# Gelu's inner polynomial: an ACT square and one fused DVE step for two POOL products and a DVE step

## The chip, the cores and the metric

The kernel runs on one core of a Trainium2 chip. The metric is the device time of one execution in microseconds; lower is better. The engines of the core are named as in the profile: PE (TensorE, matmuls), DVE (VectorE), ACT (ScalarE), POOL (GpSimd) and SP (SyncE, which issues the DMAs). Each runs its own queue of instructions in order, and they wait for each other by semaphores.

## The reference, cut to what matters

Sixteen sequences of 512 tokens of width 128 pass a causal attention with 16 heads of 8, a residual and a layer norm. Then a router picks 63 of the 512 tokens of each sequence; for them alone a second attention and a gelu MLP run, the results go back to their places, and a second layer norm ends it. The change touches only the gelu of that MLP, in its tanh form:

```python
def _gelu(x):
    return jax.nn.gelu(x, approximate=True)
...
        x1 = x_sel + o
        x2 = x1 + jax.nn.gelu(rmsnorm(x1, ln2) @ w1) @ w2
```

With h = rmsnorm(x1, ln2) @ w1, the gelu is 0.5 h (1 + tanh(sqrt(2/pi) (h + 0.044715 h^3))). The inner polynomial is h + 0.044715 h^3 = h (1 + 0.044715 h^2).

## The kernel before

The sixteen sequences are batches, taken two by two as eight pairs. One pass of the main loop is one pair and has 16 slots, 8 groups of heads for each batch of the pair. In a slot ACT takes the Tanh of one group's scores in two units out of PSUM (L708) and the Exp of the group before (L723); POOL multiplies the Exp's diagonal blocks by a triangle, the causal mask (L619, two instructions per group); PE computes the scores one group ahead (L1170) and, when four groups are masked, their products with v (L1187), which are also what frees the buffers of `pr` that the Exp writes. `pr` holds five groups, and six from pair 3 on (`SIX_FROM`, L43; the wait is at L720).

Everything else is fitted into these slots from order lists written out by hand, one for each engine (`PE_ORDER`, `VE_ORDER`, `POOL_ORDER`, `ACT_ORDER`), with two entries per slot. An entry such as `att.hh@-2` is a step of the pair two passes back. `run_side` (L479) issues them. The stages are `prep` (transposes, q, k, v and their norms, for the batch ahead), `fin` (the end of the first attention), `route`, `sel` (gather of the chosen tokens), `att` (second attention and the MLP up to the gelu) and `late` (second matmul of the MLP, scatter, last norm, for a pair up to three passes back). With the last groups of scores the first loop is empty, and the last two pairs' `sel`, `att` and `late` remain.

The steps around the change, in the order of their data:

- `att.w1` on PE (L1371) writes h to PSUM; `att.h` on DVE copies it to `hb` (L1079).
- `att.hh` on POOL: `hq` = h h. It is the first of two entries of slot 8 in POOL's list (L155), behind that slot's causal mask.
- `att.hp` on DVE: `hq` = 0.044715 `hq` + 1 (L1083). In DVE's list it stands behind `att.h` and behind `late.root2`, the four small steps L803 to L806 on the 128x8 tile `lo_v` (L134).
- `att.hu` on POOL: `hu` = `hq` h. It waits too for the second matmul of the pair before (`late.w2`), which reads `hu`.
- `att.tanh` on ACT (L694), in slot 9 behind the two Tanh units and ahead of the Exp (L175): `hq` = tanh(sqrt(2/pi) `hu`).
- `att.g` on DVE (L1087): `hu` = (`hq` + 1) h; then `late.w2` on PE (L1378) and `late.proc` on DVE (L1093, L1095).

Between `att.hp` and `att.g` DVE has `prep.qk1` (L825), `route.w` (L918, L919) and `late.norm` (eight steps, L1113); behind `att.g` come `route.row`, `route.win` (L934), `route.coef` (L956, L958), `fin.yU1`, `late.proc`, and `prep.v`, the copy of v (L836). POOL's product `prep.sq` on the next batch (`st<-qk`) follows two slots after `att.hu`. `hq` shares its memory with the tile `sc`, under whose name the profile lists it; all of POOL's plain products have the line L621.

## Time and profile before

| | us |
|---|---|
| runs | 793.32, 791.93, 792.43 |
| median | 792.43 |
| profiled execution | 795.73 |
| its span, first to last instruction | 793.9 |
| PE busy | 650.0 |
| DVE busy | 596.5 |
| ACT busy | 553.3 |
| POOL busy | 386.2 |

The busy time of an engine is the sum of its instructions; the span holds a start of some 40 us, in which weights come in and the first batch is prepared, some 650 us in which groups of scores run, and some 105 us at the end without scores. Idle time in front of an instruction is listed with the instruction that ended it. An engine's idle time matters only where the chain of work that ended last passes through it, so the chain is read beside the waits.

### The profile page before, as it was taken

The page shows a single profiled execution, that of the slowest core. Times are in us where ns is not written, and L with a number is a line of the kernel's source. Part 1 is how long each engine was busy: PE and PEld are TensorE (multiplying, and loading weights), DVE is VectorE, ACT ScalarE, POOL GpSimd, SP SyncE. Part 2 cuts the span into 40 slices and gives each one's busy share as a digit, 9 for nine tenths or more (in the row PEclk, how much of TensorE's full clock was granted, in tenths as well). Part 3 has the DMA queues.
Part 4 walks back from the last instruction along what each step waited for, and adds up shares of the span by engine and source line. Part 5 has one row for each costly group of instructions (what it writes and reads, how often), then busy time and mean ns, then how long its engine had stood idle before and what let it go on. Part 6 is the DMA issues. An engine that isn't in the chain of part 4 may idle for free.

```text
span 793.9 us, 16532 instructions
## 1 busy us (share of the span) xinstructions
PE 650.0 (82%) x6384; PEld 373.9 (47%) x6384; DVE 596.5 (75%) x1649; ACT 553.3 (70%) x403; POOL 386.2 (49%) x399
## 2 busy tenths in 40 slices
PE   3387777889989998999989998999899979855742
PEld 2243323455546454555546454545464546344432
DVE  3651636765897889888988898788998887687656
ACT  0399887786988798879788978788798969500000
POOL 5244545536555475556646564556547653511210
PEclk9558667778989998899889988898999878965755
DMA  6303030405230323040412121030303040000001
GB/s 199 67 2 80 12 69 1 81 2 107 81 80 2 69 66 82 28 67 15 66 44 53 30 53 55 19 64 4 64 28 68 2 68 28 14 1 28 0 1 53
DMA packets 97855, 36.72 MB, mean 46 GB/s; under 512 B 69090, under 2 KB 95090, under 8 KB 97778
## 3 DMA queue, kind: packets, MB, share of 16 engines
q1 hardware_dynamic: 97778, 35.67, 20.4%
q8 instruction: 51, 0.84, 0.4%
q14 instruction: 26, 0.21, 0.1%
HBM read 14.69 MB, written 4.19 MB: 24 GB/s over the span
## 4 chain that ended last, share of the span: by engine, by line
PE 45%; DVE 27%; ACT 12%; issue 9%; POOL 4%; DMA 2%; SPq 1%; DVEq 0%; ACTq 0%; POOLq 0%
PE ps_y L1187 15%; PE ps_s L1170 10%; ACT pr L723 8%; ACT th L708 4%; PE ps_m L1286 3%; DVE wins L934 2%; POOL pr L619 2%; DVE qn_v L842 2%; PE ps_m L1371 1%; PE ps_a L1236 1%; PE ps_a L1218 1%; DVE v_aug L836 1%; DMA k_st<-st 1%; PE ps_m L1270 1%; PE ps_m L1194 1%
## 5 line engine op out<-in xcount | busy, mean ns | idle before, releaser
L708 ACT ACTIVATE th<-ps_s 128x1024 f32<-128x1024 f32 (+1 forms) x256 | 278.6, 1129 | 77.1 <-PE ps_s L1170 67.5
L619 POOL TENSOR_TENSOR pr<-pr,tri 128x320 f32<-128x320 f32 (+1 forms) x256 | 188.2, 757 | 192.9 <-ACT pr L723 192.8
L723 ACT ACTIVATE pr<-th 128x2304 f32<-128x2304 f32 x128 | 271.5, 2122 | 8.7 <-PE ps_y L1187 8.4
L1170 PE MATMUL ps_s<-q_st,k_st 32*64 32x512 f16 (+7 forms) x2048 | 190.8, 315 | 42.5 <-ACT th L708 34.6
L1187 PE MATMUL ps_y<-pr,v_aug 128*32 128x512 f32 (+7 forms) x2048 | 171.6, 469 | 7.8 <-POOL pr L619 7.6
L1170 PEld LDWEIGHTS ps_s<-q_st,k_st 32*64 32x64 f16 x2048 | 92.1, 114 | 168.0 <-issue 63.5
L633 POOL TENSOR_TENSOR st<-qk,st 128x1024 f16<-128x1024 f32 x32 | 76.7, 2417 | 49.5 <-DVE st L852 49.5
L1187 PEld LDWEIGHTS ps_y<-pr,v_aug 128*32 128x32 f32 x2048 | 58.3, 116 | 76.7 <-issue 47.6
L621 POOL TENSOR_TENSOR k_wide<-qkT,head_of 128x1024 f32<-128x1024 f32 x16 | 30.1, 1901 | 41.6 <-DVE qkT L1017 41.6
L694 ACT ACTIVATE sc<-hu 128x512 f32<-128x512 f32 x8 | 5.0, 630 | 64.3 <-POOL hu L621 64.3
L934 DVE SCALAR_TENSOR_TENSOR wins<-w_wide,x,later 128x512 f16<-128x512 f32 (+1 forms) x64 | 41.2, 644 | 2.6
L690 ACT ACTIVATE pm<-pm 128x1008 f32<-128x1008 f32 x8 | 8.3, 1043 | 41.9 <-DVE pm L1031 41.9
L621 POOL TENSOR_TENSOR z_base<-x,coef 128x512 f32<-128x512 f32 x16 | 17.1, 1067 | 41.4 <-DVE coef L958 41.4
L621 POOL TENSOR_TENSOR r<-x,rw_row 128x512 f32<-128x512 f32 x16 | 18.9, 1181 | 35.5 <-DVE x L910 35.5
L621 POOL TENSOR_TENSOR st<-qk 128x1024 f32<-128x1024 f32 x16 | 30.3, 1893 | 5.9 <-DVE qk L825 5.7
L825 DVE COPY qk<-ps_a 128x512 f32<-128x512 f32 x16 | 10.7, 666 | 28.9 <-PE ps_a L1218 28.9
L1286 PE MATMUL ps_m<-mask_a,E 128*64 128x512 f32 x112 | 31.0, 605 | 0.0
L1348 PE MATMUL ps_a<-vv,k_wide 128*128 128x32 f32 x128 | 19.7, 315 | 9.2 <-DVE v_aug L836 5.7
L860 DVE STREAM_TRANSPOSE y_u<-ps_y 128x512 f32<-128x512 f32 x32 | 22.6, 705 | 5.8 <-PE ps_y L1187 5.8
L1218 PE MATMUL ps_a<-wT,xT 128*128 128x256 f32 x64 | 25.1, 532 | 0.0
L1348 PEld LDWEIGHTS ps_a<-vv,k_wide 128*128 128x128 f32 x128 | 18.9, 234 | 11.1 <-issue 6.9
L825 DVE COPY qk<-ps_m 128x512 f32<-128x512 f32 x16 | 11.1, 691 | 14.7 <-PE ps_m L1218 14.6
(224 smaller groups left out, 1074.0 us busy)
## 6 DMA issues: line engine op xcount, KB each, us to landing
x_in<-in_L_attn_x SPq DMA_DIRECT2D x16, 256.0 KB, 3.5
x_res<-in_L_attn_x SPq DMA_DIRECT2D x16, 256.0 KB, 2.8
result<-y_out SPq DMA_DIRECT2D x16, 256.0 KB, 2.2
mask_a<-in_L_ffn_attention_mask SPq DMA_DIRECT2D x3, 1024.0 KB, 5.4
pr<-in_L_ffn_attention_mask SPq DMA_DIRECT2D x2, 1024.0 KB, 7.9
w_sb<-in_L_ffn_w SPq DMA_DIRECT2D x2, 256.0 KB
q_st<-st SPq DMA_TRANSPOSE x16, 4.5
k_st<-st SPq DMA_TRANSPOSE x16, 4.8
```

The lines of the kernel that those rows point to most:

```text
L619: return nc.gpsimd.tensor_tensor(buf, buf, tri[:, None, :].to_broadcast([P, blocks, 64]), ALU.mult)
L621: mul = lambda out, a, b: nc.gpsimd.tensor_tensor(out, a, b, ALU.mult)
L633: pl["prep"].done(nc.gpsimd.tensor_tensor(lo_parts[s], qk_twice[s], hi_parts[s], ALU.subtract), f"lo_{part}", b)
L708: nc.scalar.activation(th[:, gi % 2, c0:c1], ps_s[:, c0:c1], ACT.Tanh, scale=1.0 / (QK_SCALE ** 2 * DH ** 0.5 * SOFTCAP))\
L723: nc.scalar.activation(pr[:, probs_at(n):probs_at(n) + GROUP], th[:, gi % 2, :], ACT.Exp, scale=SOFTCAP).then_inc(exp_done, 1)
L860: ve["fin"].done(nc.vector.transpose(y_u[:, half], ps_y[:, :]), f"yU{half}", b)
L934: step(lambda: nc.vector.scalar_tensor_tensor(won[c], w_wide[:, P * c:], x1[:, k, c, D:D + 1], later[:, 0:n], ALU.is_le, ALU.mult, accum_o ...
L1170: last = mm(ps_s[64 * s:64 * s + 64, COL[kb]:COL[kb] + S - 64 * kb], k_st[rows, k, gi // 2, 64 * kb:64 * kb + 64], q_st[rows, k, gi // 2, ...
L1187: last = mm(ps_y[32 * j:32 * j + 32, 64 * kb:S], v_aug[:, k, kb, gi, :], pr[:, c:c + S - 64 * kb], start=(kb == 0), stop=(kb == NB - 1), s ...
L1218: last = mm(at(f"prep.qk{i}", b)[:, :].rearrange("p (n t e) -> p n t e", t=2, e=32)[:, :, t % 2], xT[:, P * t:P * t + P], wT[:, 0:2, :].re ...
L1286: last = mm(at("sel.R")[SLOTS * k:SLOTS * k + SLOTS, :], E[:, c, SLOTS * k:SLOTS * k + SLOTS], (mask_b if k and q < 2 else mask_a)[:, c, : ...
L1348: last = mm(at("att.PV")[:, 32 * n:32 * n + 32], PT[:, n, :], vv[:, n, :, :].rearrange("p k c -> p (k c)"), start=True, stop=True)
```

## The change

The two POOL steps `hh` and `hu` and the DVE step `hp` are taken out. ACT gets a step `sq` in slot 9, directly ahead of its Tanh: `hq` = Square(h), as soon as `h` is there. DVE gets a step `u` where `hp` stood: `hu` = (`hq` + 1/0.044715) h, one instruction, which waits for the square and, as `hu` did on POOL, for the second matmul of the pair before. The factor 0.044715 goes into the scale of the Tanh. No other entry of an order list is moved.

```diff
     "att": ["sc0", "mx0", "sub0", "sc1", "mx1", "sub1", "den", "rden", "PT0", "PT1", "o0", "o1", "oT", "x1f",
-        "ss2"] + rsqrt_of("r2", 1) + rsqrt_of("r2", 2) + ["hn2", "h2T", "h", "hp", "g"],
+        "ss2"] + rsqrt_of("r2", 1) + rsqrt_of("r2", 2) + ["hn2", "h2T", "h", "u", "g"],
     "late": ["x2", "proc", "z0", "z1"] + moments_of(2 * NT, "_") + rsqrt_of("ln_", 1) + rsqrt_of("ln_", 2) +
...
     "sel": ["zb0", "zb1"],
-    "att": ["kw0", "kw1", "hh", "hu"],
+    "att": ["kw0", "kw1"],
 }
...
     ["att.root1@-2", "route.rank/0@-1"], ["prep.qk0/0@1", "att.root2@-2", "att.hn@-2", "fin.root2/1@-1"],
-    ["att.h2T@-2", "fin.x1/1@-1", "fin.yU0/0@0"], ["att.h@-2", "late.root2@-3", "att.hp@-2"],
+    ["att.h2T@-2", "fin.x1/1@-1", "fin.yU0/0@0"], ["att.h@-2", "late.root2@-3", "att.u@-2"],
     ["prep.qk1/0@1", "route.w/1@-1"], ["late.norm@-3", "att.g@-2", "route.row/1@-1", "route.win/1@-1"],
...
     ["route.xw/1@-1"], [],
-    ["att.hh@-2"], ["att.hu@-2"],
+    [], [],
     [], [],
...
     [], [],
-    [], ["att.tanh@-2"],
+    ["att.sq@-2"], ["att.tanh@-2"],
     [], [],
...
         gate_ready = sem("gate_ready")
+        square_ready = sem("square_ready")
         turned = [sem(f"turned{i}") for i in range(2)]
...

-            def att_hh(q, _):
-
-                ve["att"].wait(pool, q, "h")
-                pl["att"].done(mul(hq[:, :], hb[:, :], hb[:, :]), "hh", q)
-
-            def att_hu(q, _):
-                pe["late"].wait(pool, q - 1, "w2")
-                ve["att"].wait(pool, q, "hp")
-                pl["att"].done(mul(hu[:, :], hq[:, :], hb[:, :]), "hu", q)
-
-            table = {"prep.sq": prep_sq, "prep.lo": prep_lo, "route.xw": route_xw, "sel.zb": sel_zb, "att.kw": att_kw,
-                     "att.hh": att_hh, "att.hu": att_hu}
+            table = {"prep.sq": prep_sq, "prep.lo": prep_lo, "route.xw": route_xw, "sel.zb": sel_zb, "att.kw": att_kw}

...

+            def att_sq(q, _):
+                ve["att"].wait(act, q, "h")
+                nc.scalar.activation(hq[:, :], hb[:, :], ACT.Square).then_inc(square_ready, 1)
+
             def att_tanh(q, _):
-                pl["att"].wait(act, q, "hu")
-                nc.scalar.activation(hq[:, :], hu[:, :], ACT.Tanh, scale=float(np.sqrt(2.0 / np.pi)))\
+                ve["att"].wait(act, q, "u")
+                nc.scalar.activation(hq[:, :], hu[:, :], ACT.Tanh, scale=float(0.044715 * np.sqrt(2.0 / np.pi)))\
                     .then_inc(gate_ready, 1)

-            table = {"att.exp": att_exp, "att.tanh": att_tanh}
+            table = {"att.exp": att_exp, "att.sq": att_sq, "att.tanh": att_tanh}

...

-            def att_hp(q, _):
-                pl["att"].wait(v, q, "hh")
-                ve["att"].done(nc.vector.tensor_scalar(hq[:, :], hq[:, :], 0.044715, 1.0, ALU.mult, ALU.add), "hp", q)
+            def att_u(q, _):
+                v.wait_ge(square_ready, q + 1)
+                pe["late"].wait(v, q - 1, "w2")
+                ve["att"].done(nc.vector.scalar_tensor_tensor(hu[:, :], hq[:, :], 1.0 / 0.044715, hb[:, :], ALU.add, ALU.mult),
+                               "u", q)

...
                      "att.oT": att_oT, "att.x1f": att_wo, "att.ss": att_squares, "att.hn": att_hn, "att.h2T": att_h2T,
-                     "att.h": att_w1, "att.hp": att_hp, "att.g": att_gate, "late.proc": late_w2,
+                     "att.h": att_w1, "att.u": att_u, "att.g": att_gate, "late.proc": late_w2,
                      "late.z0": lambda q, _: late_sc(q, 0), "late.z1": lambda q, _: late_sc(q, 1), "late.ln": late_ln,
```

## Rows read from the trace of the kernel before

**Rows 1.** The page: busy us, share of the span and instructions of each engine

```profile
PE 650.0 (82%) x6384; PEld 373.9 (47%) x6384; DVE 596.5 (75%) x1649; ACT 553.3 (70%) x403; POOL 386.2 (49%) x399
```

**Rows 2.** Busy time by stretch, from gelu Tanh to gelu Tanh, pairs 2 and 3

```profile
core 0: us, PE busy (x) PEld busy (x) DVE busy (x) ACT busy (x) POOL busy (x), PEclk, DMA share, GB/s
...
408.50:490.40 81.90, 76.05 (x801) 43.81 (x805) 71.82 (x205) 68.61 (x50) 47.07 (x47) 0.90 0.21 47
490.40:574.50 84.10, 75.97 (x805) 43.07 (x805) 72.75 (x205) 68.62 (x51) 47.05 (x47) 0.90 0.19 42
```

**Rows 3.** Busy time by stretch, around the gelu Tanh of pairs 2 and 4

```profile
406.00:416.70 10.70, 10.70 (x144) 5.68 (x145) 10.00 (x31) 7.98 (x7) 4.65 (x6) 0.91 0.18 54
...
571.50:582.40 10.90, 10.07 (x141) 5.61 (x141) 10.43 (x31) 7.72 (x6) 5.06 (x6) 0.99 0.17 50
```

**Rows 4.** Groups of ACT by line and form: busy us, mean ns | idle before, releaser

```profile
L723 ACT ACTIVATE pr<-th 128x2304 f32<-128x2304 f32 x128 | 271.5, 2122 | 8.7 <-PE ps_y L1187 8.4
...
L694 ACT ACTIVATE sc<-hu 128x512 f32<-128x512 f32 x8 | 5.0, 630 | 64.3 <-POOL hu L621 64.3
...
L708 ACT ACT_TABLE_LOAD x1 | 1.3, 1283 | 0.0
```

**Rows 5.** The instructions on tile `sc` (`hq`): duration ns min/median/max, first and last start

```profile
L621 POOL TENSOR_TENSOR sc<-hb x8: 1029/1037/1042, 241.3 to 773.0; 128x512 f32<-128x512 f32 x8
L1083 DVE TENSOR_SCALAR sc<-sc x8: 420/420/427, 242.3 to 774.4; 128x512 f32<-128x512 f32 x8
L621 POOL TENSOR_TENSOR hu<-sc,hb x8: 1261/1267/1277, 242.8 to 775.0; 128x512 f32<-128x512 f32 x8
...
L1087 DVE SCALAR_TENSOR_TENSOR hu<-sc,hb x8: 677/684/691, 244.8 to 777.8; 128x512 f32<-128x512 f32 x8
```

**Rows 6.** The same view of tile `lo_v`, a step of `late.root2`

```profile
L804 DVE SCALAR_TENSOR_TENSOR lo_v<-lo_v x8: 166/963/1035, 323.5 to 788.4; 128x8 f32<-128x8 f32 x8
```

**Rows 7.** Timeline of pair 2: start us, us, engine, line, what [idle before <-releaser]

```profile
404.38 0.69 DVE L1079 COPY hb<-ps_m 128x512 f32<-128x512 f32 x1 [1.06 <-PE ps_m L1371]
...
408.32 0.23 DVE L919 TENSOR_SCALAR x<-x,rb 128x4 f32<-128x4 f32 x1
...
408.46 2.14 DVE L1113 TENSOR_SCALAR y_out<-y_out,mv,lo_v 128x128 f32<-128x128 f32 x8
408.54 0.63 ACT L694 ACTIVATE sc<-hu 128x512 f32<-128x512 f32 x1 [3.50 <-POOL hu L621]
...
411.26 1.87 POOL L619 TENSOR_TENSOR pr<-pr,tri 128x320 f32<-128x320 f32 x2 [2.75 <-ACT pr L723]
...
416.69 1.41 DVE L836 COPY v_aug<-ps_m 64x512 f32<-64x512 f32 x2 [0.23 <-PE ps_m L1226]
416.88 1.89 POOL L621 TENSOR_TENSOR st<-qk 128x1024 f32<-128x1024 f32 x1
```

**Rows 8.** The chain that ended last, in pairs 0, 2 and 4: start, us, what

```profile
242.82 1.28 POOL hu L621
...
415.57 1.10 PE ps_m L1226 x32
...
573.18 1.29 POOL hu L621
```

**Rows 9.** The same chain in pairs 6 and 7, around the gelu

```profile
720.35 1.05 DVE lo_v L804
...
722.76 0.80 DVE x L919
...
773.04 1.05 DVE lo_v L804
...
774.82 3.02 DVE y_out L1113 x8
```

**Rows 10.** Timeline of pairs 2 and 3 where PE waits for `yT`

```profile
425.16 2.05 PE L1236 MATMUL ps_a<-wT,yT 128*128 128x128 f32 x8 [0.71 <-DVE yT L875]
...
505.94 0.85 DVE L801 TENSOR_TENSOR sel_v<-sel_v 128x1 f32<-128x1 f32 x1
...
508.10 2.05 PE L1236 MATMUL ps_a<-wT,yT 128*128 128x128 f32 x8 [1.75 <-DVE yT L875]
```

## The prediction

> **What bounds the kernel now.** I read the engines' busy times first [rows 1]: no engine is full over the whole span, PE comes nearest with 82%. So I cut the span into pairs of batches, from one gelu Tanh to the next [rows 2]. In a steady pair PE is busy 76.05 of 81.90 us, ACT 68.61, DVE 71.82, POOL 47.07. The reader should see that PE leads, that ACT has some 13 us to spare and that POOL is half empty.
>
> Then the piece that the change touches. ACT sits idle in front of every gelu Tanh: 64.3 us over eight pairs, and POOL's `hu` product ended the wait [rows 4]. In a steady pair it is 3.50 us [rows 7]. The naive reading is that eight such waits are there to be won. The next view speaks against it: from 406.0 to 416.7, which begins inside the stall of pair 2, PE is busy 10.70 of 10.70 us [rows 3]. PE has score groups computed ahead and other work to do, and does not notice that ACT stands still. The chain of work that ended last says the same: there it runs through PE (the `v` matmuls at 415.57) and not through `hu` [rows 8]. It passes through `hu` in only two of the first six pairs, pair 0 (242.82) and pair 4 (573.18) [rows 8], and in pair 4 PE does have holes, 10.07 busy of 10.90 [rows 3]. In the last two pairs no scores are left, the chain runs step by step on DVE, and there the gelu is on it [rows 9].
>
> **The change part by part.** Removed per pair: POOL's `hh` (1037 ns) and `hu` (1267 ns), DVE's `hp` (420 ns) [rows 5]. Added: on ACT a Square over 128x512, on DVE the fused step `u` with two SBUF inputs.
>
> Square is not in the trace. Its lower bound is the Tanh of the same shape, 630 ns; Tanh and Exp lie on one line, (2122 - 630) / (2304 - 512) = 0.833 ns a column [rows 4], so I take 0.63. The upper bound is a table load of 1.28 before it and another before the Tanh [rows 4]; one such load covers all Tanh and Exp so far, and the third rival below takes that up. A gain below 0.63 is excluded by that line. `u` has the form of `g` (the step that applies the gate), 684 ns [rows 5]; against `hp` DVE pays 0.26 us more.
>
> Chain from `h` to the Tanh in pair 2: `h` ends at 404.38 + 0.69 = 405.07, the Tanh starts at 408.54, so 3.47 us [rows 7]. After: Square 0.63, `u` 0.68, and three hand-overs of some 0.06 each, 1.5 us. The Tanh comes 1.9 us sooner; ACT's wait of 3.50 becomes two short ones of 0.9 us together, with the 0.63 of Square inside the old wait.
>
> The Square stands in ACT's queue where the Tanh stood, one entry ahead. Behind it are the Tanh and the next Exp, as before; nothing is queued longer than now. POOL is moved past nothing: its next mask waits for an Exp. No DMA is touched. The wait for `w2` of the pair before moves from POOL to DVE; those matmuls are over by then, because they were needed for the output of that pair: cost nothing.
>
> There is a second effect that the diff doesn't name. `hh` and `hu` slow DVE. The step L804 on 128x8 takes 166 ns at best and 963 in the median [rows 6], and it is long where it lies beside `hh` (720.35 and 773.04) [rows 9]. The same happens to the 128x4 step L919, 0.80 beside `hu` in pair 6 [rows 9] against 0.23 [rows 7], and to the eight normalising steps L1113, 3.02 beside `hu` in pair 7 [rows 9] against 2.14 in pair 2 [rows 7]. Without POOL's products these blocks are gone.
>
> Sum, by place:
> - Pair 6 (no scores left): L804 1.05 to 0.18, gain 0.87; L919 0.80 to 0.23, gain 0.57; `u` for `hp`, loss 0.26; `u` waits some 0.06 for Square. Net 1.1 us, all on the chain.
> - Pair 7: L804 0.87; L1113 3.02 to 2.14, gain 0.88; loss 0.26 and some 0.1 of wait. Net 1.4 us. The Tanh is then done before DVE gets to `g`.
> - Pairs 0 and 4: PE's holes in that stretch are 10.90 - 10.07 = 0.83 us [rows 3]. The gain lies between 0 and 0.83 each; I take 0.6, near the upper end, since the chain does run through `hu`: 1.2 us.
> - Pairs 1, 2, 3, 5: PE has no hole in the stretch, so 0. What covers it is PE's own queue; if that cover were gone, it would be 1.9 us each.
>
> Together 1.1 + 1.4 + 1.2 = 3.7 us. The profiled execution took 795.73 us (span 793.9 and 1.8 around it), 0.4% over the median of the runs, so by itself it would come to 792.0; on the median 792.43 - 3.7 = 788.7.
>
> A rule of the Trainium skill speaks against the change. ScalarE: Activation LUTs, section Rules for kernel authors, puts multiplications on VectorE and not on ScalarE. By that rule the square would be a DVE product of some 0.68 us (estimate from `g`), on the engine that carries the last two pairs, and the sum would be some 1.3 us smaller; the trace has ACT idle for 3.50 us at this place, so here the row decides for ACT.
>
> **The rivals.**
>
> *POOL's masks come earlier and block DVE (slower).* The Exp behind the gelu Tanh starts 1.9 us sooner, so POOL's next causal mask, now at 411.26 with 1.87 us, starts near 409.4 [rows 7]. Today it lies beside the `win` steps; then it lies on the normalising steps (408.46 to 410.60), which a POOL product can hold up by 0.88, as pair 7 shows. DVE then comes later to the small steps ahead of the copy of `v` at 416.69, where it has only 0.23 us of slack, and behind which POOL's product of 1.89 us waits to start [rows 7]: a DVE step that arrives just after that one has begun loses up to 1.9 us. What one collision on this chain costs is in the trace. Pairs 2 and 3 run alike until a small DVE step ahead of `yT` is held 0.85 us by a mask (505.94); PE then waits 1.75 instead of 0.71 us for `yT` [rows 10], and the pair takes 84.1 instead of 81.9 us [rows 2], 2.2 more. Four pairs (1 to 4) with such a collision: 8.8 - 3.7 = 5 us slower, 797.5. It decides once DVE is over 0.23 us late at the copy of `v`. For it: in pairs 3 to 5 `pr` has a sixth buffer, so ACT keeps its lead longer there. Against: DVE gets 0.8 us from L804 and starts the normalising some 0.4 us sooner. The Trainium skill has this as a rule (SBUF — State Buffer, section Who interferes with whom: DVE and GpSimd share one port pair, held for a whole instruction, by DVE steps with two SBUF inputs among others); by that rule the trace agrees with the long L804 rows, and `u`, with two SBUF inputs, is exposed too.
>
> *Collisions in one or two pairs only.* 1.5 x 2.2 - 3.7 is about 0: 792.
>
> *The whole lead counts.* Were ACT the bound in the steady pairs, six of them would gain 1.9 us each and the tail 2.5: 14 us, 778.5. For it: the size of the waits. Against: PE without a hole [rows 3].
>
> *Square needs its own table.* Two loads per pair: the chain from `h` to the Tanh is then about 1.28 + 0.63 + 1.28 + 0.63 = 3.8 us, no shorter than today's 3.47; only DVE's relief in the tail remains, about 791. ScalarE: Activation LUTs, section Table sets, says that cheap functions are in every set; it doesn't list Square for the set of Exp. No row here shows a Square.
>
> **How the numbers follow.** Forecast (tail and two pairs gain, steady pairs keep their period) 0.42; whole lead 0.05; collisions cancel the gain or own table, 0.21; collisions win 0.32. Some 0.2% of this kernel, 1.6 us, is what a measurement can tell from no change. Faster 0.47, same 0.21, slower 0.32. The likeliest case alone reaches from 786.8 (both holes of pairs 0 and 4 and 0.23 in the others) to 790.8 (the holes give nothing). The range with the others is 786 to 798; it leaves out the whole lead and collisions worse than one a pair.
>
> **What would show it.** Right: ACT's waits at the gelu fall from 3.5 to under 1 us; L804 on 128x8 falls to 0.17 in the median; the steady pairs stay at 81.9 us within 0.3; from the last Exp of the scores to the end the span is 2 to 3 us shorter; no table load beyond two. Wrong: steady pairs at 80 us (the lead counts), or at 83 to 84 with longer PE waits for `yT` and for the copy of `v` (collisions), or loads beside every Square.

## The result and the profile after

| | before | after |
|---|---|---|
| median us (4 runs each, same chip) | 792.18 | 816.66 |
| lowest and highest | 787.88, 793.32 | 815.57, 819.76 |
| profiled execution, its span | 795.73, 793.9 | 819.76, 818.0 |

The ratio is 1.0326, with a 95% interval from 1.0278 to 1.0374: the changed kernel is 3.3% slower, and the forecast of 788.7 had the sign wrong. The two spans differ by 24.1 us. Executions of one kernel differ too: over all the runs of this case the kernel before took 780.4 to 799.8 us, so a difference between two single executions says less than a ratio of many.

First the page of the changed kernel, busy times as in [rows 1]:

```profile
PE 678.5 (83%) x6384; PEld 397.1 (49%) x6384; DVE 599.6 (73%) x1649; ACT 558.9 (68%) x411; POOL 368.2 (45%) x383
```

POOL works 18 us less, ACT 5.6 more, as costed. PE runs the same 6384 matmuls and is busy for 28.5 us more. No PE instruction was changed, so its instructions took longer. Before that is followed, the groups of ACT, for [rows 4]:

```profile
L684 ACT ACTIVATE sc<-hb 128x512 f32<-128x512 f32 x8 | 5.0, 630 | 37.9 <-DVE hb L1073 37.8
L688 ACT ACTIVATE sc<-hu 128x512 f32<-128x512 f32 x8 | 5.0, 630 | 6.4 <-DVE hu L1078 6.4
```

L684 is the Square: 630 ns, with no table load beside it. The wait in front of the Tanh fell from 64.3 to 6.4 us in all. The 37.8 us that now stand in front of the Square are those of the last two pairs (22.08 and 15.69), where ACT has no scores left and waits for h; in front of the other six Squares it doesn't wait. What the change was to do on ACT, it does.

Then the pairs, from gelu Tanh to gelu Tanh. Before, the eight Tanh and the end cut the span into 244.1 | 82.5, 81.9, 81.9, 84.1, 80.7, 68.4, 52.7 | 17.6; after into 240.9 | 84.5, 88.7, 88.7, 88.7, 88.8, 66.9, 52.8 | 18.0. The differences, -3.2, +2.0, +6.8, +6.8, +4.7, +8.1, -1.5, +0.1 and +0.4, add up to the 24 us. All of the loss lies in the intervals from pair 0 to pair 5, 26.4 us of it in the four from pair 1 on (the 2.0 of pair 0, which has no normalising steps beside it yet, were not followed further). Pair 2 of the changed kernel, whole and in two stretches (busy time by stretch, columns as in [rows 2]):

```profile
414.11:502.81 88.70, 81.75 (x803) 48.71 (x799) 74.19 (x204) 69.35 (x51) 44.74 (x44) 0.83 0.21 43
414.11:423.30 9.19, 7.75 (x105) 4.37 (x101) 8.83 (x23) 9.01 (x8) 3.70 (x5) 1.00 0.20 61
423.30:443.80 20.50, 20.46 (x149) 14.96 (x153) 15.97 (x39) 10.50 (x7) 8.06 (x7) 0.50 0.05 13
```

Against [rows 2] PE is busy 81.75 instead of 76.05 us, 5.7 more, and idle 1.1 more. The third line shows why: for 20.5 us PE is busy without a gap at a granted clock of 0.50, which is 1.2 GHz and not 2.4. In front of that stretch PE, at full clock, stood still for 1.4 of 9.2 us. The same 20.5 us of the kernel before have a granted clock of 0.92:

```profile
417.60:438.10 20.50, 19.42 (x197) 12.46 (x199) 17.52 (x54) 15.84 (x13) 11.42 (x11) 0.92 0.32 65
```

The other three of the four pairs from 1 to 4 have such a stretch of some 20 us at the same place, from some 9 us behind the Tanh on; in the kernel before no stretch at half clock in these places is longer than 7 us. The timeline of pair 2 of the changed kernel at that place (start, us, engine, line, what, idle before and what ended it), for [rows 7]:

```profile
411.39 0.69 DVE L1073 COPY hb<-ps_m 128x512 f32<-128x512 f32 x1 [0.35 <-PE ps_m L1367]
412.63 0.63 ACT L684 ACTIVATE sc<-hb 128x512 f32<-128x512 f32 x1
413.38 0.69 DVE L1078 SCALAR_TENSOR_TENSOR hu<-sc,hb 128x512 f32<-128x512 f32 x1
414.11 0.63 ACT L688 ACTIVATE sc<-hu 128x512 f32<-128x512 f32 x1 [0.84 <-DVE hu L1078]
415.44 3.21 DVE L1109 TENSOR_SCALAR y_out<-y_out,mv,lo_v 128x128 f32<-128x128 f32 x8
416.83 1.48 POOL L620 TENSOR_TENSOR pr<-pr,tri 128x320 f32<-128x320 f32 x2 [3.79 <-ACT pr L717]
...
421.08 1.75 POOL L620 TENSOR_TENSOR pr<-pr,tri 128x320 f32<-128x320 f32 x2 [2.77 <-ACT pr L717]
422.80 1.93 POOL L622 TENSOR_TENSOR st<-qk 128x1024 f32<-128x1024 f32 x1
422.91 0.28 DVE L950 TENSOR_REDUCE edge<-ps_m 128x1 f32<-128x128 f32 x1
423.30 1.46 DVE L952 TENSOR_SCALAR coef<-x,edge 128x4 f32<-128x4 f32 x1
423.34 1.97 PE L1222 MATMUL ps_m<-wT,xT 128*64 128x64 f32 x32 [1.47 <-DVE edge L950]
426.19 1.40 DVE L830 COPY v_aug<-ps_m 64x512 f32<-64x512 f32 x2
```

And two lines of the kernel before, the read of `edge` and the `v` matmuls:

```profile
414.39 0.29 DVE L956 TENSOR_REDUCE edge<-ps_m 128x1 f32<-128x128 f32 x1
...
415.50 1.15 PE L1226 MATMUL ps_m<-wT,xT 128*64 128x64 f32 x32
```

The reader should follow four things. The mask (L620) begins 1.39 us after the eight normalising steps (L1109), inside them; in [rows 7] it begins 2.80 us after, when they are over. They take 3.21 us and not 2.14, and the next mask lies on the `win` steps. So `edge` is read 11.52 us after the start of h; in the kernel before it is read 10.01 us after (414.39 and 404.38). PE's `v` matmuls write to the bank of PSUM that this read sets free: they wait 1.47 us, where before they came 0.82 us after the read. Behind the wait the clock is at half, the matmuls take 1.97 and not 1.15 us, and ACT later waits for scores: 17.3 us in this pair, against 8.4 before. Pairs 1, 3 and 4 of the changed kernel run the same way, with waits of 1.47, 1.48 and 1.32 us.

At the end of the kernel the timeline of pairs 6 and 7 has what was forecast from [rows 9], from the copy of h to the gate step:

```profile
745.13 0.69 DVE L1073 COPY hb<-ps_m 128x512 f32<-128x512 f32 x1 [1.14 <-PE ps_m L1367]
750.03 0.69 DVE L1083 SCALAR_TENSOR_TENSOR hu<-sc,hb 128x512 f32<-128x512 f32 x1
...
797.89 0.69 DVE L1073 COPY hb<-ps_m 128x512 f32<-128x512 f32 x1 [2.17 <-PE ps_m L1367]
801.94 0.68 DVE L1083 SCALAR_TENSOR_TENSOR hu<-sc,hb 128x512 f32<-128x512 f32 x1
```

These are 4.90 and 4.05 us; before they were 5.97 (719.55 to 725.52) and 5.53 (772.24 to 777.77).

### The profile page after: what moved, and what is told of

The parts are those of the page before. It is cut to its first block, busy times and chain, and to the rows that moved or that the text cites. A ratio compares the mean times of both kernels' runs of the same rounds, so it can differ in the third digit from the quotient of the medians.

```text
span 818.0 us, 16524 instructions
## 1 busy us (share of the span) xinstructions
PE 678.5 (83%) x6384; PEld 397.1 (49%) x6384; DVE 599.6 (73%) x1649; ACT 558.9 (68%) x411; POOL 368.2 (45%) x383
## 4 chain that ended last, share of the span: by engine, by line
PE 52%; DVE 23%; ACT 13%; issue 7%; POOL 3%; DMA 1%; SPq 0%; DVEq 0%; ACTq 0%
PE ps_y L1183 15%; PE ps_s L1166 12%; ACT pr L717 9%; ACT th L702 4%; PE ps_m L1282 4%; PE ps_m L1266 3%; DVE wins L928 2%; DVE y_out L1109 2%; POOL pr L620 2%; PE ps_m L1367 2%; PE ps_a L1232 2%; PE ps_a L1383 1%; PE ps_m L1383 1%; PE ps_m L1222 1%; PE ps_m L1190 1%
## 5 line engine op out<-in xcount | busy, mean ns | idle before, releaser
L620 POOL TENSOR_TENSOR pr<-pr,tri 128x320 f32<-128x320 f32 (+1 forms) x256 | 188.2, 757 | 220.2 <-ACT pr L717 220.2
L1166 PE MATMUL ps_s<-q_st,k_st 32*64 32x512 f16 (+7 forms) x2048 | 198.7, 325 | 38.5 <-ACT th L702 28.7
L1183 PE MATMUL ps_y<-pr,v_aug 128*32 128x512 f32 (+7 forms) x2048 | 168.2, 462 | 9.9 <-POOL pr L620 9.6
L1166 PEld LDWEIGHTS ps_s<-q_st,k_st 32*64 32x64 f16 x2048 | 94.2, 116 | 166.2 <-issue 70.6
L684 ACT ACTIVATE sc<-hb 128x512 f32<-128x512 f32 x8 | 5.0, 630 | 37.9 <-DVE hb L1073 37.8
L1266 PE MATMUL ps_m<-x,E 128*64 128x129 f32 x128 | 28.2, 391 | 0.1
L986 DVE TENSOR_SCALAR hnT<-ps_a,g 128x256 f32<-128x256 f32 x8 | 3.9, 484 | 27.2 <-PE ps_a L1296 27.2
```

The lines of the kernel that those rows point to most:

```text
L620: return nc.gpsimd.tensor_tensor(buf, buf, tri[:, None, :].to_broadcast([P, blocks, 64]), ALU.mult)
L1166: last = mm(ps_s[64 * s:64 * s + 64, COL[kb]:COL[kb] + S - 64 * kb], k_st[rows, k, gi // 2, 64 * kb:64 * kb + 64], q_st[rows, k, gi // 2, ...
L1183: last = mm(ps_y[32 * j:32 * j + 32, 64 * kb:S], v_aug[:, k, kb, gi, :], pr[:, c:c + S - 64 * kb], start=(kb == 0), stop=(kb == NB - 1), s ...
L1266: mm(at("sel.gather")[rows, 0:D + 1], E[:, c, rows], x1[:, k, c, :], start=(c == 0), stop=(c == NT - 1))
```

## The experiments

The theory after the result: ACT's earlier Exp brings POOL's mask onto DVE's normalising steps; DVE is then late at `edge`; PE stops at the `v` matmuls; the clock falls behind the stop. Each link has an experiment. A table of all runs stands first; the kernel before ran beside each (793.0, 793.9, 792.5, 792.6 and 792.4 us in the five groups). "Pairs" are the four Tanh-to-Tanh intervals 1 to 4 of the profiled execution; where that execution lay over 5 us from the median, its time stands beside them. In e17_tail these four pairs are those of the kernel before, unchanged, so its row shows how far one interval moves by itself: by 1 to 2 us. The mean of the four is 82.15 us in the kernel before and 88.75 in the changed one.

| run | us | ratio to before, 95% interval | pairs, us |
|---|---|---|---|
| before | 792.2 | 1 | 81.9, 81.9, 84.1, 80.7 |
| after | 816.7 | 1.033 (1.028 to 1.037) | 88.7, 88.7, 88.7, 88.8 |
| e1_hold_exp | 793.8 | 1.002 (0.998 to 1.007) | 83.9, 82.1, 82.1, 82.4 |
| e9_mask_waits | 797.1 | 1.003 (1.001 to 1.006) | 84.4, 83.2, 84.5, 83.1 |
| e11_fill | 800.5 | 1.006 (1.003 to 1.010) | 82.7, 84.3, 82.6, 82.7 |
| e4_norm_behind | 812.9 | 1.026 (1.021 to 1.031) | 86.7, 90.8, 86.7, 91.0 (818.1) |
| e5_v_later | 816.9 | one run | 85.1, 89.2, 86.3, 90.9 |
| e6_sq_later | 811.5 | one run | 84.8, 88.7, 84.4, 84.3 |
| e7_before_late1 | 829.1 | 1.045 (1.038 to 1.051) | 85.1, 88.9, 88.8, 88.9 |
| e8_before_late2 | 812.3 | 1.023 (1.017 to 1.028) | 85.3, 85.3, 85.5, 85.6 |
| e10_wait_sq | 809.3 | 1.028 (1.017 to 1.040) | 84.7, 85.2, 85.3, 85.5 |
| e12_before_sq | 819.6 | 1.042 (1.032 to 1.051) | 87.2, 86.4, 87.7, 86.4 |
| e13_late1_sq | 824.0 | 1.047 (1.037 to 1.057) | 87.2, 86.4, 87.7, 86.4 |
| e3_act_square | 790.7 | 1.000 (0.993 to 1.007) | 80.0, 83.6, 82.0, 79.5 (782.6) |
| e2_pool_square | 808.4 | 1.021 (1.015 to 1.027) | 85.4, 85.4, 87.2, 89.3 |
| e14_before_fill | 800.1 | 1.008 (1.005 to 1.011) | 82.1, 82.1, 83.3, 83.7 |
| e15_e3_fill | 793.3 | 1.002 (0.999 to 1.005) | 81.2, 81.2, 83.8, 82.9 |
| e16_e9_fill | 806.8 | 1.019 (1.014 to 1.024) | 86.4, 85.9, 85.4, 85.5 |
| e17_tail | 790.4 | 0.996 (0.993 to 0.998) | 80.4, 80.3, 82.8, 81.9 |
| e18_e3_tail | 789.3 | 0.995 (0.992 to 0.998) | 79.5, 84.1, 80.8, 80.0 (782.5) |

### First link: the mask on the normalising steps

**Holding the Exp back.** The changed kernel with three small squares more on ACT.

```diff
                     .then_inc(gate_ready, 1)
+                for i in range(3):
+                    act.wait_ge(held, 3 * q + i)
+                    nc.scalar.activation(pr[:, 6 * GROUP:6 * GROUP + 256], later[:, 0:256], ACT.Square).then_inc(held, 1)
```

> The changed kernel with three small ACT squares of a constant added behind the gelu Tanh (their results are used by nobody), some 1.4 us a pair, so that the Exp behind it and with it POOL's next mask come as late after h as in the kernel before. Theory (the mask comes too early and meets DVE's eight normalising steps; PE then waits for DVE and its clock falls): more work on ACT makes it faster, steady pairs fall from 88.7 to 81.5 to 82.5 us, the normalising steps take 2.14 instead of 3.21, time 787 to 794. Rival (the new round trip DVE to ACT to DVE costs the time, whenever the mask comes): 814 to 820, pairs stay at 88 to 89.

793.83 us: more work on ACT gives 23 us back. The timeline of pair 2 has the steps whole and the mask behind them:

```profile
409.95 2.14 DVE L1113 TENSOR_SCALAR y_out<-y_out,mv,lo_v 128x128 f32<-128x128 f32 x8
412.55 1.44 POOL L621 TENSOR_TENSOR pr<-pr,tri 128x320 f32<-128x320 f32 x2 [5.00 <-ACT pr L721]
```

**Moving the mask alone.** Holding the Exp delays all of ACT behind it, so this run leaves ACT as it is.

```diff
+                        if s == 9:
+                            ve["late"].wait(pool, p - 3, "o7_")
                         causal(b.no * 8 + gi, 0, 512, 5)
```

> The changed kernel, but POOL's causal mask of slot 9 waits for the normalising steps of DVE (the mask is moved by some 0.8 us; the Square, the early Tanh and the early Exp on ACT stay). Theory (the mask on the normalising steps makes DVE late, PE stops for 1.5 us at the v matmuls and the granted clock falls behind the stop): the eight steps take 2.14 us and not 3.2, the read of edge comes 10.4 us after h and not 11.5, PE's stop at the v matmuls is under 0.4 us, the steady pairs take 82 us; 788 to 797. Rival (what comes behind is enough by itself: the next mask on the win steps, POOL's product on st beside coef): the stop stays over 1 us, 805 to 818.

797.12 us, 0.1 above the theory's range and 8 below the rival's. The stop at the `v` matmuls is 0.59, 0.16, 0.59 and 0.36 us in pairs 1 to 4, so not under 0.4 in all of them, and the pairs take 83.8 us in the mean, not 82. Timeline of pair 2:

```profile
410.09 2.14 DVE L1111 TENSOR_SCALAR y_out<-y_out,mv,lo_v 128x128 f32<-128x128 f32 x8
412.37 1.74 POOL L620 TENSOR_TENSOR pr<-pr,tri 128x320 f32<-128x320 f32 x2 [4.92 <-DVE y_out L1111]
...
417.09 1.15 PE L1224 MATMUL ps_m<-wT,xT 128*64 128x64 f32 x32 [0.16 <-DVE edge L952]
417.15 1.89 POOL L622 TENSOR_TENSOR st<-qk 128x1024 f32<-128x1024 f32 x1
419.04 1.40 DVE L832 COPY v_aug<-ps_m 64x512 f32<-64x512 f32 x2
...
420.54 1.07 PE L1268 MATMUL ps_m<-x,E 128*64 128x129 f32 x8 [0.72 <-issue]
```

One mask moved by under a microsecond is worth some 20 us: the loss against the kernel before, as run beside each, falls from 24.5 to 3.2 us. The last three lines show part of what is left: the copy of `v` begins where POOL's product on `st` ends, and PE stops 0.72 us.

**Moving the normalising steps instead.** They go behind the first `win` group in DVE's list.

```diff
-    ["prep.qk1/0@1", "route.w/1@-1"], ["late.norm@-3", "att.g@-2", "route.row/1@-1", "route.win/1@-1"],
+    ["prep.qk1/0@1", "route.w/1@-1"], ["att.g@-2", "route.row/1@-1", "route.win/1@-1", "late.norm@-3"],
```

> The changed kernel with DVE's eight normalising steps moved from ahead of the gate to behind the win steps; ACT and POOL keep the early mask. Theory: the mask now lies on the win steps (0.2 to 0.5 us) and not on the normalising ones, DVE reads the thr bank some 0.9 us sooner, PE's wait of 1.47 us ahead of the v matmuls falls under 0.5, the clock stays up, pairs 81.5 to 84, time 786 to 800. Rival (POOL's long product st<-qk in front of coef is the cause, 1.46 us): coef is held as before, time 805 to 818.

812.92 us: missed. The time is in the rival's range, but not for the rival's reason: `coef` took 0.23 us. The steps met the next mask and the product on `st` instead, took 4.58 us, and still stood ahead of the read of `edge`:

```profile
413.98 4.58 DVE L1109 TENSOR_SCALAR y_out<-y_out,mv,lo_v 128x128 f32<-128x128 f32 x8
418.90 1.87 PE L1222 MATMUL ps_m<-wT,xT 128*64 128x64 f32 x30 [2.41 <-DVE edge L950]
```

So the edit made the lateness larger, and the expectation of the theory rested on a place for the steps that wasn't free.

**Which part of the change does it.** The two halves, each alone: the Square on ACT with `hp` on DVE and `hu` on POOL kept; and `hh` on POOL kept, with the fused step `u` on DVE.

```diff
-                pl["att"].done(mul(hq[:, :], hb[:, :], hb[:, :]), "hh", q)
...
+                nc.scalar.activation(hq[:, :], hb[:, :], ACT.Square).then_inc(square_ready, 1)
```

The first is the kernel before with this edit; the second is the changed kernel with this edit undone.

> One part of the change alone: the square goes to ACT, the polynomial step stays on DVE (0.42 us) and the product with h stays on POOL (1.27 us). The Tanh then comes some 3.25 us after the start of h (4.16 in the kernel before, 2.72 in the changed one), and the normalising steps begin some 0.8 us sooner too, since the product hh is gone from POOL. Theory (what counts is the mask against the normalising steps): the mask begins 2.7 us after them, they take 2.14 us, no stop at the v matmuls: 786 to 797. Rival (any lead of ACT at this place costs): 803 to 818.

> The other part of the change alone: h h stays on POOL (1.04 us), the fused step goes to DVE (0.69 us), nothing is added to ACT. The Tanh comes some 3.0 us after the start of h (4.16 before, 2.72 changed), and the normalising steps some 0.3 us later than in the kernel before, so the mask of slot 9 begins some 1.4 us after their start, as in the changed kernel, and not 2.8. Theory (mask against the normalising steps): they take 2.8 to 3.3 us, edge is read late, PE stops at the v matmuls or for E: 803 to 825. Rival (it is the square on ACT that costs): 788 to 797.

790.74 and 808.36 us, both inside the theory's ranges. The timelines of pair 2, first the Square alone, then the fused step alone:

```profile
399.80 2.14 DVE L1113 TENSOR_SCALAR y_out<-y_out,mv,lo_v 128x128 f32<-128x128 f32 x8
402.60 1.88 POOL L620 TENSOR_TENSOR pr<-pr,tri 128x320 f32<-128x320 f32 x2 [2.75 <-ACT pr L723]
```

```profile
413.27 3.20 DVE L1114 TENSOR_SCALAR y_out<-y_out,mv,lo_v 128x128 f32<-128x128 f32 x8
414.65 1.48 POOL L620 TENSOR_TENSOR pr<-pr,tri 128x320 f32<-128x320 f32 x2 [3.78 <-ACT pr L722]
...
421.16 1.06 PE L1227 MATMUL ps_m<-wT,xT 128*64 128x64 f32 x29 [1.05 <-DVE edge L955]
```

What matters is not how early ACT is, but how early against DVE: with the Square alone the mask begins 2.80 us after the normalising steps, as in the kernel before; with the fused step alone 1.38 us, as in the changed one. With the Square alone the Tanh and the normalising steps move together: they start 3.26 and 3.18 us after h, against 4.16 and 4.08 in the kernel before. With the fused step alone only the Tanh moves: 2.87 and 4.21 us. The Square on ACT shows no loss (ratio 1.000, 0.993 to 1.007); the fused step alone costs most of what the whole change costs.

### Second link: DVE late by itself

One useless reduce on DVE in the kernel before, ahead of the gate step; two in the second run (`range(2)`).

```diff
             def att_gate(q, _):
+                for i in range(1):
+                    nc.vector.tensor_reduce(idle[:, 4 * q + i:4 * q + i + 1], hb[:, :], AX.X, ALU.add)
```

> The kernel before, with one useless reduce of 128x512 (some 0.68 us) on DVE ahead of the gate step of each pair: DVE is late by that much and nothing else changes on ACT, POOL or PE. In the kernel before PE comes to the v matmuls 0.82 us after edge was read (414.68 and 415.50), so there is no stop there. Theory (a threshold: the price comes with a stop of PE at the v matmuls): 0 to 0.45 a pair and 1.4 at the end, 793 to 797. Rival (every microsecond of DVE counts, no threshold): 0.68 for eight pairs, 798.

> The same with two reduces, 1.36 us. Theory: DVE is past the slack of 0.82 us, PE stops for some 0.5 us at the v matmuls, the clock falls behind it, 3 to 7 us in each of the steady pairs, and 2.7 at the end: 808 to 830. Rival (lateness counts one to one, a short stop does not bring the clock down): 8 x 1.36 less the slack, 797 to 804.

829.07 and 812.34 us. The first is far outside what either theory gave, the second is in the range of the theory; and the larger lateness costs less. Timeline of pair 2 with one reduce, and the row of the stretch behind it:

```profile
419.99 1.90 POOL L622 TENSOR_TENSOR st<-qk 128x1024 f32<-128x1024 f32 x1
421.90 1.40 DVE L837 COPY v_aug<-ps_m 64x512 f32<-64x512 f32 x2
423.40 1.95 PE L1273 MATMUL ps_m<-x,E 128*64 128x129 f32 x8 [1.83 <-issue]
```

```profile
423.40:440.40 17.00, 17.00 (x98) 12.12 (x102) 11.86 (x33) 8.92 (x7) 7.34 (x7) 0.52 0.12 24
```

The slack that counted was the 0.23 us at the copy of `v` [rows 7]. In the kernel before the copy begins 0.19 us ahead of POOL's product; here DVE came after it, the copy waited for the whole product (419.99 + 1.90 = 421.89), PE stopped 1.83 us for the matmuls of E (at the `v` matmuls only 0.25), and 17 us at half clock followed, in pairs 2, 3 and 4 and not in pair 1. With two reduces PE stops 0.79 us at the `v` matmuls and 1.55 for E, and the copy of `v` waits for the product there too, but in pair 2 the clock stays at 1.00 behind these stops, and the next stretch at half clock, behind a later stop, is some 3.5 us long. These pairs take 85.4 us all the same, 3.3 more than before: the lateness costs something by itself, and the long stretch at half clock, where it comes, costs more. The length of the stop doesn't decide whether it comes.

### Third link: the stop and the clock

**Filling the stop.** The changed kernel with five useless matmuls in front of the second matmul of the MLP. DVE, ACT and POOL keep their collisions.

```diff
                 bank_free("late.w2", q)
+                for c in range(5 if q < 6 else 0):
+                    mm(at("late.w2")[:, 0:D], hu[:, 0:P], w2_sb[:, 0, :], start=True, stop=True)
```

> The changed kernel, with five useless matmuls (128x128, 0.29 us each at full clock, 1.45 in all) ahead of the second matmul of the MLP in the six pairs of the loop, so that PE works in the 1.47 us in which it stood still ahead of the v matmuls. DVE, ACT and POOL do what they do in the changed kernel, the collisions stay, and the v matmuls start no sooner. Theory (the stop costs little by itself; the price is the slow clock behind it, some 5.8 us a pair): the clock stays at 1.0 behind it and four to five pairs fall by 4 to 6 us: 790 to 800. Rival (the lateness of DVE sets the period, the clock is a symptom): 814 to 822.

800.51 us, 0.5 above the theory's range and 13 below the rival's. Timeline of pair 2: the normalising steps are as long as in the changed kernel, and the stop is filled to 0.36 us.

```profile
410.96 3.21 DVE L1109 TENSOR_SCALAR y_out<-y_out,mv,lo_v 128x128 f32<-128x128 f32 x8
...
418.86 0.82 PE L1222 MATMUL ps_m<-wT,xT 128*64 128x64 f32 x21 [0.36 <-DVE edge L950]
```

The row of the stretch from these matmuls on has a granted clock of 0.92 and not 0.50:

```profile
418.82:439.32 20.50, 17.44 (x190) 11.23 (x190) 17.05 (x41) 13.38 (x10) 9.84 (x8) 0.92 0.12 28
```

Useless work on PE gave back most of the loss: against the kernel before, as run beside each, it fell from 24.5 to 6.6 us, with DVE as late at `edge` as in the changed kernel (7.48 us behind the start of the normalising steps, there 7.47).

**What the half clock costs, inside one run.** POOL's product on `st` one slot later in the changed kernel, meant to free `coef` (it took 0.23 us then and not 1.46).

```diff
     [], [],
+    [], [],
     ["prep.sq/0@1"], [],
-    [], [],
     ["prep.lo/0@1"], [],
```

> The changed kernel with POOL's product st<-qk one slot later, behind one more mask, so that it can't hold coef. Theory (PE waits for thr, which DVE does ahead of coef): coef falls from 1.46 to 0.25 us, but PE's wait ahead of the v matmuls and the low clock stay, time 808 to 820. Rival (the lock on coef is what counts): pairs 82 to 84, time 785 to 800.

811.47 us, as expected: the stop doesn't hang on that product. The gain of this run is another one. In pairs 2 and 3 PE stops equally long, 1.32 us, at the `v` matmuls. The two lines of the timeline:

```profile
425.30 1.89 PE L1222 MATMUL ps_m<-wT,xT 128*64 128x64 f32 x32 [1.32 <-DVE edge L950]
513.97 1.83 PE L1222 MATMUL ps_m<-wT,xT 128*64 128x64 f32 x32 [1.32 <-DVE edge L950]
```

And the rows of the 20.5 us behind each (the second in two pieces):

```profile
425.50:446.00 20.50, 20.50 (x149) 14.79 (x150) 16.29 (x38) 10.70 (x8) 9.24 (x7) 0.50 0.06 15
514.00:521.00 7.00, 7.00 (x78) 5.67 (x79) 5.79 (x11) 5.66 (x5) 3.26 (x3) 0.51 0.00 1
521.00:534.50 13.50, 12.38 (x127) 8.01 (x128) 12.13 (x33) 8.44 (x7) 6.03 (x4) 1.00 0.10 27
```

20.5 us at half clock once, 7.0 us the other time. The pairs take 88.7 and 84.4 us: 13.5 us of half clock cost 4.3 us here. In pair 1 of the same run the stop is longer, and the clock behind it stays at 1.00:

```profile
340.69 1.15 PE L1222 MATMUL ps_m<-wT,xT 128*64 128x64 f32 x32 [1.48 <-DVE edge L950]
```

The three pairs without the long stretch take 84.48 us in the mean, 2.3 more than the 82.15 of the kernel before. So the 6.6 us a pair of the changed kernel divide into some 2.3 for the lateness and 4.3 for the long stretch. That is an estimate from one profiled execution; the 2.3 is near what one interval moves by itself, the 4.3 is not.

**The stop moved.** The `v` matmuls behind the next step in PE's list.

```diff
-    ["route.thr/0@-1"], ["late.w2@-2", "prep.v/0@1"],
-    ["route.won/1@-1"],
+    ["route.thr/0@-1"], ["late.w2@-2"],
+    ["route.won/1@-1", "prep.v/0@1"],
```

> The changed kernel with one PE step moved: the v matmuls of the next batch (L1222) go behind the next unit of scores and the won matmuls, so that PE has other work while DVE is late. POOL, ACT and DVE keep their lists. Theory (DVE is late by about 1.5 us, and PE's wait there lets the clock fall): the wait shrinks under 0.5 us, the clock of the 19 us behind it goes from 0.50 to 0.85 or more, pairs 82 to 85, time 790 to 803. Rival (the clock falls for another reason, or DVE's lateness itself sets the period): pairs stay at 87 to 89, time 808 to 820.

816.87 us: missed, in the rival's range. The next step on PE (`won`, L1245) needs a bank that DVE reads behind `coef` (L1089, 424.97 to 425.22 in pair 2), so it waits for the same chain and stops longer: it starts at 425.32, with 2.70 us of idle time in front of it. With two of the pairs at 89 to 91 us the rival's second reading, that the lateness of DVE sets the period, isn't refuted by this run; the run with the filled stop speaks against it.

**Filling the stops of the other kernels.** Useless matmuls in the three places where PE stands still in every pair: seven ahead of `h2T`, three ahead of the scores of the second attention, three (in the last run six) ahead of the `wo` matmuls. They are put into the kernel before, the one with the Square alone, and the changed one with the mask moved.

```diff
+            def fill(use, unit, n):
+                bank_free(use, unit)
+                for i in range(n):
+                    mm(at(use, unit if isinstance(unit, Batch) else None)[:, 0:P], ident[:, :], ident[:, :], start=True, stop=True)
```

> The kernel before, with useless matmuls (128x128, 0.29 us at full clock) where PE stands still in every pair of the loop: seven in the wait for ACT ahead of h2T (a stop of 2.3 us), three ahead of the first scores of the second attention (0.94) and three ahead of the wo matmuls of the batch that waits for yT (0.71). Behind each of these stops the kernel before has a stretch of 3.5 to 7 us at half the clock, some 17 us a pair. Theory (the slow clock follows the stops and sets the pair's length through PE): the slow stretches shrink to less than half, the pairs fall by 2 to 5 us until DVE (71.8 busy of 81.9) is next: 765 to 785. Rival (the slow clock does not follow the stops, or DVE and ACT hold the period anyway): 789 to 800.

> The same useless matmuls in the kernel that has only the square on ACT (790.7 without them). Theory: 763 to 785. Rival: 788 to 800.

> The same in the changed kernel with the mask of slot 9 behind the normalising steps (797.1 without them), six ahead of the wo matmuls, where it stops 1.9 us. Theory: 768 to 788. Rival: 792 to 803.

800.12, 793.28 and 806.76 us: the rival, in all three, the first 0.1 and the last 3.8 above its range. The granted clock of pair 2 of the kernel before rose from 0.90 to 0.95, and the pair did not get shorter:

```profile
410.26:492.36 82.10, 76.08 (x827) 45.57 (x823) 72.79 (x205) 68.74 (x50) 47.31 (x46) 0.95 0.25 47
```

So a stretch at half clock is no cost of its own. It costs where PE's matmuls are on the chain that ended last and nothing else is nearly as long. In pair 2 of the changed kernel that chain runs through PE alone from the `v` matmuls (423.34) to 446.81, past the end of the stretch at half clock. In the kernel before it runs through DVE beside the stretch from 462.5 to 469. At the end of that pair (482.7 to 490) PE at half clock is on it; but in the kernel with the useless matmuls, where the clock is up there, DVE's steps and POOL's `hu` are on it, and the Tanh comes no sooner. One piece of each, in this order:

```profile
423.34 1.97 PE ps_m L1222 x32
...
463.88 0.94 DVE qn_v L806
...
491.05 1.29 POOL hu L621
```

### What POOL's product on `st` allows

The product was next in line after the mask was moved; three runs move it one slot later (the diff of e6): with the mask moved, in the kernel before, and there with one reduce.

> The changed kernel with the mask of slot 9 behind the normalising steps, and POOL's product on st (1.89 us) one slot later. With the mask moved alone the copy of v began only when the product on st was over (8.40 + 1.89 us after the Tanh, copy at 10.29), and PE stopped 0.7 us for E and 1.9 us for yT. Theory (that product ahead of the copy of v is the second link, in the place of the mask on the normalising steps): the copy of v begins at 8.3 to 8.6 us after the Tanh, both stops shrink, the pairs take 80.5 to 82 us: 783 to 791. Rival (the product only meets another step of DVE later): pairs of 82 to 84, 792 to 799.

> The kernel before with POOL's product on st one slot later and nothing else. There the copy of v begins 0.19 us ahead of that product, so by the theory nothing is to be had: 790 to 795. Rival (the product is in the way in the kernel before too): 780 to 788; or it meets steps ahead of yT: 796 to 805.

> The kernel before with DVE late by one reduce (0.68 us, which alone made 829 us) and POOL's product on st one slot later. In the run with the reduce alone the copy of v began at 10.26 us after the Tanh, where the product on st ended, and not at 8.15, and PE stopped 1.83 us for E with the slow clock behind. Theory (0.68 us was past the 0.23 us of slack at the copy of v, and the product does the rest): without the product there the copy begins at 8.9, PE's stop for E is under 0.5 us, 793 to 800. Rival (the lateness itself is enough): 812 to 830.

809.34, 819.63 and 824.0 us. All three missed the theory's range; the first two lie above their rivals' ranges too, and the third lies in its rival's. The second is what the others needed as a control, and it decides: the move alone costs 27 us, so the other two say little on the time. Pair 2 of the kernel before with that move:

```profile
436.04 1.22 DVE L842 TENSOR_REDUCE qn_v<-st 128x128 f32<-128x1024 f32 x1 [4.22 <-POOL st L621]
439.32 0.97 PE L1387 MATMUL ps_m<-x,ET 64*128 64x128 f32 x3 [3.64 <-DVE xs L974]
```

DVE's list has the reduce of the product ahead of other steps; it now waits 4.22 us, and PE 3.64 us behind it. In the run with the reduce the copy of `v` did begin at 8.89 us after the Tanh and the stop for E fell to 0.48, as expected, but the time is no nearer, with this new wait in their place. One slot later the product takes more than it gives.

### Keeping the part that held

The change in the last two pairs alone, where no masks are left; over the kernel before, and over the one with the Square alone.

```diff
...
+                if q < 6:
+                    act.wait_ge(cube_ready, q + 1)
+                else:
+                    ve["att"].wait(act, q, "h")
+                    nc.scalar.activation(hq[:, :], hb[:, :], ACT.Square).then_inc(square_ready, 1)
+                    ve["att"].wait(act, q, "hp")
...
```

> The kernel before in the six pairs of the loop, the change (square on ACT, fused step on DVE) in the last two pairs alone, where no scores and no masks are left. Theory (the two tail terms of the prediction, 1.1 and 1.4 us, are real and on the path that sets the end): 1.5 to 3 us under the kernel before, 789.5 to 791 against 792.5. Rival (they are given back behind the gate step): within 1 us of it.

> The same tail, with only the square on ACT in the six pairs of the loop (POOL's product with h and DVE's polynomial step kept there). The square on ACT alone gave 790.7, no difference from the kernel before. Theory: 1.5 to 4 us under the kernel before, 787 to 791. Rival: within 1 us.

790.42 and 789.34 us. The ratios 0.9957 (0.9933 to 0.9981) and 0.9947 (0.9919 to 0.9976) are 3.4 and 4.2 us less than before, with intervals that leave out no change: both beat both kernels. In the first of them the last two pairs take 4.90 and 4.04 us from h to the gate step, as in the changed kernel. So a gain of about the size of the two tail terms reaches the end. That each term does so is not shown: from the gate step of pair 6 to the copy of h of pair 7, where nothing was changed, the profiled executions take 46.72 us before, 48.26 in e17_tail and 45.65 in e18_e3_tail, a spread as large as the terms. Between the two versions the runs show no difference.

## Why the prediction was wrong

**What held.** Square takes 0.63 us and needs no table; `u` takes 0.69 (0.68 was put); ACT's wait fell to 0.84 us a pair (under 0.9); the tail terms are 1.07 and 1.48 us from h to the gate step (1.1 and 1.4), and the change in the tail alone is worth some 3.4 us (1.5 to 5.3). Two signs did not come. L804 (now L798) fell to 0.34 us in the median and not to 0.17. And from the end of the last Exp the changed kernel takes 104.4 us against 105.2, not 2 to 3 less: from the gate step of pair 6 to the copy of h of pair 7 it loses 1.1 again (47.86 against 46.72).

**The step that failed** is the line on pairs 1, 2, 3 and 5: no hole of PE in the stretch, so 0, and "what covers it is PE's own queue". The intervals from pairs 1, 2 and 3 lost 6.8, 6.8 and 4.7 us, and that from pair 4, put down for a gain of 0.6, lost 8.1; that from pair 5 lost nothing. The view was right for what PE waits for ACT [rows 3], but the question was what else the earlier Exp moves. The cover of PE's own queue reaches as far as the `v` matmuls, which need a DVE step, the read of `edge`. In the kernel before PE came there 0.82 us after that read (414.39 + 0.29 and 415.50); in the changed one the read is 1.5 us later against h, and the cover is gone.

**The first rival named it.** The mask on the normalising steps, their price (0.88 put, 1.07 measured), the late small steps and the lock by the product on `st` are in the trace as written there; `coef`, held for 1.46 us, is the step that arrives just after the product has begun. Two of its numbers were wrong. The price was taken as 2.2 us from one collision in [rows 10], where the clock came back after some 7 us; the four intervals lost 26.4 us instead of 8.8, of which the long stretch at half clock is the larger part (4.3 of 6.6 a pair, by the run that has pairs with it and without). The rest, some 2.3 a pair, is near the price that was put. So 797.5 stood for what came out at 816.7, and the range ended at 798. (The bounds of the likeliest case don't follow from its terms: 2.5 + 2 x 0.83 + 4 x 0.23 is 5.1 and gives 787.4, and the 2.5 of the tail alone gives 789.9, where 786.8 and 790.8 were put. That decided nothing.) The place was wrong too: PE stopped at the bank of `edge`, before the copy of `v`; the 0.23 us there did count, as the run with one reduce shows, but were not reached first.

**What spoke against that rival did not come.** DVE was to get 0.8 us from L804 and to start the normalising some 0.4 us sooner. It started 4.05 us after h, and 4.08 before (415.44 - 411.39, and [rows 7]). In pair 2 L798 takes 0.52 us where L804 took 0.96, but L797 ahead of it takes 0.52 and not 0.36, since a mask (411.63, 1.41 us) now lies on both, and `u` costs 0.27 us more than `hp`. ACT gained 1.4 us against h and DVE nothing: that difference is the collision. This could have been worked out from [rows 7] by placing the mask against the start of the steps in both kernels, which the runs with half of the change then showed to be the deciding number (2.80 or 1.4 us).

**The rule.** These rows show a DVE step held by a POOL product that began first: `coef` 1.46 us for 0.23, and one of the eight normalising steps 0.90 to 1.06 us for 0.34. The Trainium skill, SBUF — State Buffer, section Who interferes with whom, says this of the port pair that the two engines share: whoever issues first has it for the whole instruction. The prediction cited that rule for the rival and gave the rival 0.32; the rows of pairs 1 to 4 bear the rule out. The other rule, ScalarE: Activation LUTs, section Rules for kernel authors (multiplications belong on VectorE), would have kept the Square off ACT; the run with the Square alone shows no loss by it.

**What stays open.** Why the clock stays at half for 20.5 us behind one stop of 1.32 us, for 7.0 behind another of the same length at the same place, and not at all behind one of 1.48 us there, all in one run. For this reason the loss of a late DVE can't be computed from its lateness: 0.68 us cost 35 us and 1.36 us cost 18.

## What to carry to other kernels

Before an engine is made faster, place what it triggers against the other engines' steps with times relative to one common event, before and after; a gain on one engine without the same gain on its neighbour is a shift, and a shift can move a lock onto a chain. A stop of PE of 1.5 us can cost several times its length, so cost a rival that ends in such a stop by the longest stretch at half clock that a trace shows, not by a short one. Here the trace of the kernel before had one of 17.3 us (643.1 to 660.4, granted clock 0.51, PE idle for 2.8 of them), beside those of 3 to 7 us that the price came from. Where a change gains in one stage and collides in another, make it in the first alone.

## What was not expected of the hardware

- PE can be busy for 20.50 of 20.50 us and have a granted clock of 0.50 for all of them, behind a stop of 1.32 us; in the next pair of the same run the clock was back after 7.0 us, and in the pair before it stayed at 1.00 behind a stop of 1.48.
- Useless matmuls in a stop kept the clock up (0.92 instead of 0.50 behind the `v` matmuls of the changed kernel) and gave 16 us back there (816.7 to 800.5); in the kernel before they raised that of a pair from 0.90 to 0.95, and the time rose by 0.8%.
- A DVE step on 128x4 took 1.46 us beside a POOL product of 1.93 us, and 0.23 without it.
